# A mixture-of-experts decoder: who sends the transfers of the expert stage, and in which order

## The reference, cut to what matters

```
logits = x @ gate_w.T                       # 1024 tokens x 64 experts
topk_w, topk_idx = top_k(softmax(logits), 8)
for e in range(64):                         # w13[e]: 256 x 256, w2[e]: 256 x 128
    g = x @ w13[e][:128].T
    u = x @ w13[e][128:].T
    o = (silu(g) * u) @ w2[e].T
    out = out + combine[:, e] * o           # combine: topk_w where e was chosen
x = layernorm(x + out)
```

## Time and profile before

| | |
|---|---|
| time, median of 3 runs | 886.04 us (884.73 to 886.28) |
| profiled execution | 880.95 us, span 879.3 us |
| mean granted TensorE clock in it | 0.961 of full speed |
| PE busy | 791.1 us, 90% |
| ACT busy | 385.3 us, 44% |
| expert stage, first to last transposes of rows | 630.4 to 831.0 us |

### The profile page before, as it was taken

One profiled execution on the slowest core, in us unless ns is written; L12 is line 12 of the kernel. 1 busy time (PEld: TensorE's weight loads), 2 busy tenths in 40 slices (PEclk: granted clock), 3 DMA queues, 4 the chain that ended last, 5 costly groups with the idle time before them and its releaser, 6 DMA issues.

```text
span 879.3 us, 17480 instructions
## 1 busy us (share of the span) xinstructions
PE 791.1 (90%) x5756; PEld 663.4 (75%) x5763; DVE 547.4 (62%) x1778; ACT 385.3 (44%) x1147; POOL 322.8 (37%) x399
## 2 busy tenths in 40 slices
PE   6999998988999999999959998983399999899958
PEld 4677776766898989898936776662299999799846
DVE  2877777854666666666684688773166666555514
ACT  3445545532443434343426766651144444344434
POOL 1121112121232121212112367777366666566611
PEclk8999999999999999999987999996599999999979
DMA  9534400001121213120003244722358999955373
GB/s 257 146 115 138 132 9 13 7 1 37 43 85 42 84 44 111 43 66 25 13 10 111 72 150 139 260 81 102 116 169 287 303 297 292 323 166 167 117 308 129
DMA packets 62680, 110.16 MB, mean 125 GB/s; under 512 B 11243, under 2 KB 41433, under 8 KB 61312
## 3 DMA queue, kind: packets, MB, share of 16 engines
q1 hardware_dynamic: 40464, 73.14, 26.0%
q10 hardware_dynamic: 12960, 18.57, 6.9%
q0 software_dynamic: 9168, 17.35, 5.4%
HBM read 94.50 MB, written 35.52 MB: 148 GB/s over the span
## 4 chain that ended last, share of the span: by engine, by line
PE 79%; DVE 5%; DMA 5%; issue 4%; POOL 4%; ACT 2%; SPq 1%; DVEq 0%; POOLq 0%
PE ps L165 72%; PE ps L168 6%; DMA rows_e<-x_slots 2%; POOL x_slots L1493 2%; DMA dnb_sb<-in_dnb 1%; POOL y_slots L1854 1%; DMA rowso<-y_slots 1%; DVE topc L1382 1%; DVE pTc L1394 0%; SPq L1697 0%; DVE stats L1043 0%; DVE oT L1024 0%; ACT o_hi L961 0%; DMA x_slots<-rows_all,index_all 0%; DVE x_all L1040 0%
## 5 line engine op out<-in xcount | busy, mean ns | idle before, releaser
L1854 POOL DMA_INDIRECT y_slots<-o_e,index_e x127 | 125.0, 984 | 87.2 <-issue 58.8
L165 PE MATMUL ps<-xT_e,w_slot 128*128 128x128 f32 x760 | 100.6, 275 | 0.3 <-ACT xT_e L1793 0.2
L165 PEld LDWEIGHTS ps<-xT_e,w_slot 128*128 128x128 f32 x760 | 92.4, 192 | 1.0 <-ACT xT_e L1793 0.5
L165 PEld LDWEIGHTS ps<-diagc,softc 128*128 128x128 f32 x512 | 64.1, 204 | 33.8 <-POOL diagc L1502 24.2
L1835 DVE TENSOR_TENSOR h_e<-ps,gate_e 128x128 f32<-128x128 f32 x127 | 37.0, 291 | 81.1 <-ACT gate_e L1799 81.1
L1793 ACT COPY xT_e<-ps 128x256 f32<-128x256 f32 x127 | 47.3, 372 | 79.6 <-PE ps L168 77.7
L1340 ACT ACTIVATE softc<-ps,topc 128x256 f32<-128x256 f32 x128 | 59.0, 476 | 47.1 <-DVE topc L1382 41.5
L165 PE MATMUL ps<-diagc,softc 128*128 128x128 f32 x512 | 70.3, 294 | 8.6 <-DVE pTc L1394 4.9
L168 PE MATMUL ps<-ident,rows_e 128*128 128x128 f32 x254 | 49.7, 278 | 25.2 <-DMA rows_e<-x_slots 24.6
L1493 POOL DMA_INDIRECT x_slots<-rows_all,index_all x64 | 63.8, 997 | 18.0 <-issue 15.9
L168 PEld LDWEIGHTS ps<-ident,rows_e 128*128 128x128 f32 x254 | 35.4, 143 | 38.9 <-DMA rows_e<-x_slots 27.0
(11 more groups left out here) (271 smaller groups left out, 1869.8 us busy)
## 6 DMA issues: line engine op xcount, KB each, us to landing
w_slot<-in_we SPq DMA_DIRECT2D x71, 384.0 KB
rows_e<-x_slots SPq DMA_DIRECT2D x69, 136.0 KB
w_slot<-in_we ACTq DMA_DIRECT2D x24, 384.0 KB
x_slots<-blank SPq DMA_DIRECT2D x4, 2176.0 KB, 8.9
rowso<-y_slots SPq DMA_DIRECT2D x8, 1024.0 KB, 13.1
rows_e<-x_slots ACTq DMA_DIRECT2D x58, 136.0 KB
w_kept<-in_we SPq DMA_DIRECT2D x20, 384.0 KB, 4.3
wh<-in_wqkv SPq DMA_DIRECT2D x16, 384.0 KB, 3.6
```

The lines of the kernel that those rows point to most:

```text
L165: return self.pe.matmul(out, lhsT, rhs, start=start, stop=stop, skip_group_check=shared)
L1854: pool.indirect_dma_start(m.y_slots, bass.IndirectOffsetOnAxis(ap=T.index[:, :], axis=0), T.o[:, :], None, bounds_check=TOK * TOPK - 1, oo ...
```

## The change

All issues of the expert stage move to SP. ACT waits for no transfer of its own and sends nothing. SP's loop goes over the tiles: at j it sends the rows of tile j+5, whatever the kind, and then the weights whose buffer is freed by tile j-4 or earlier (`+ 4 <= j`), whatever the kind. The plan is waited for by the first issue that needs a register (`line_of`), and a register, once loaded, is used for both transfers of the tile.

```diff
-AHEAD = 8
...
@@ sp_experts
     for j in range(WORK):
         load_rows(t, sp, j, own_rows(m, j))
-    sp.wait_ge(*tp.lines_set(1))
-    todo = [j for j in LOADS if ORDER[j] >= NE]
-    for j in range(PLANNED - 3, TILES):
-        while todo and LOADS[LOADS.index(todo[0]) - SLOTS] + AHEAD <= j:
+
+    def line_of(j):
+
+        if j not in place:
+            if not place:
+                sp.wait_ge(*tp.lines_set(1))
+            place[j] = sp.value_load(r.extra_row[0:1, ORDER[j] - NE:ORDER[j] - NE + 1])
+        return place[j]
+
+    todo = LOADS[SLOTS:]
+    for j in range(1, TILES + 1):
+        ahead = j - 1 + WORK
+        if ahead < TILES and ORDER[ahead] < NE:
+            load_rows(t, sp, ahead, own_rows(m, ahead))
+        elif ahead < TILES:
+            at = line_of(ahead)
+            load_rows(t, sp, ahead, m.x5_slots[bass.ds(at, P), :], cond=at < NE * ROWS)
+        while todo and LOADS[LOADS.index(todo[0]) - SLOTS] + 4 <= j:
             k = todo.pop(0)
-            at = place[k] = sp.value_load(r.extra_row[0:1, ORDER[k] - NE:ORDER[k] - NE + 1])
-            load_weights(t, sp, k, a["we"][bass.ds(at // ROWS, 1), :, :].rearrange("a p n -> (a p) n"), cond=at < NE * ROWS)
-        if ORDER[j] >= NE:
-            at = place.pop(j)
-            load_rows(t, sp, j, m.x5_slots[bass.ds(at, P), :], cond=at < NE * ROWS)
+            if ORDER[k] < NE:
+                load_weights(t, sp, k, own_weights(a, k))
+            else:
+                at = line_of(k)
+                load_weights(t, sp, k, a["we"][bass.ds(at // ROWS, 1), :, :].rearrange("a p n -> (a p) n"), cond=at < NE * ROWS)
...
@@ act_experts
-def act_experts(m, a, t, tc):
-
+def act_experts(m, t):
     act = m.act
     act.preload_act_table(ACT.Silu)
-    for k in range(PARTS):
-        act.wait_ge(*tc.row_out[k](NSEQ * TOPK // PARTS))
-    todo = [j for j in LOADS[SLOTS:] if ORDER[j] < NE]
     for j in range(TILES + 1):
...
-        ahead = j - 1 + WORK
-        if WORK <= ahead < TILES and ORDER[ahead] < NE:
-            load_rows(t, act, ahead, own_rows(m, ahead))
-        while todo and LOADS[LOADS.index(todo[0]) - SLOTS] + 5 <= j:
-            k = todo.pop(0)
-            load_weights(t, act, k, own_weights(a, k))
```

More of the change, by code:

```diff
@@ L1992, in program_pe, with program_act @@
     pe_combine(m, s.to, s.te)
-def program_act(m, a, s, out):
+def program_act(m, s, out):
     act_layer0(m, s.t0, s.t1)
@@ L1999, in program_act @@
     act_cross1(m, s.tc, s.r, s.t1)
-    act_experts(m, a, s.te, s.tc)
+    act_experts(m, s.te)
     act_combine(m, s.to, s.te, s.r, out)
@@ L2060, in decoder @@
         program_pe(m, s)
-        program_act(m, a, s, out)
+        program_act(m, s, out)
         program_dve(m, s)
```

## The result

The changed kernel takes 881.61 us (median of 6 runs, 878.16 to 883.3), the one before 886.16 us on the same chips (6 runs). The ratio is 0.995, 95% interval 0.9927 to 0.9972: faster, by 2.5 to 6.5 us. The forecast was 884.5 with a range from 882.2 to 888.2: right in direction, too small in size, and outside the range. The direction was no strong claim either: "faster" had a chance of 0.41, "same" 0.42.

What follows compares the result with a forecast made beforehand. PE bounds the kernel, so transfers count only where PE stands; the expert stage loses 5.8 us. Plan's wait +1.4, dense stretch -2.1 and end -0.8 give -1.5 us: 884.5 from a median of 886.04, range 882.2 to 888.2.

Steps and rivals of the forecast that it cites:

- The plan's wait: Tile 15: its rows wait on SP behind the plan; stall 2.0 us, net +1.4 without tile 20's 0.6.
- The catch-up behind it: Tiles 16 to 20: rows regain their lead after tile 15's stall; slack grows from tile 17, tile 20 no longer waits.
- The dense stretch: Tiles 69 to 86: issues some 2.5 us earlier cut stalls of 3.4 us to 1.3, a gain of 2.1.
- the queue grows by 0.45 us each: Dense stretch: for 12 tiles transfers outlast PE's step, adding 5.4 us to a 4.3 us load, leaving a 1.5 us stall.
- The rate of 333 GB/s: Dense stretch: DMA rate at full share, giving 2.0 us for a tile's 0.66 MB against 1.55 us of PE.
- full gain: Rival, chance 0.19: dense stretch needs no wait (3.4), end gives 0.8, tile 15 stalls 1.7; -3.1 us, 882.9.
- bytes bind: Rival, chance 0.15: DMA bytes keep the dense stretch's stalls, only tile 15's shows anew; +0.6 us, 886.6.
- The end: Late in the expert stage: a long step at 815 (0.3) and a wait for ACT's copy at 824.82 (0.5) go; gain 0.8.
- The sum: Whole kernel: plan's wait +1.4, dense stretch -2.1, end -0.8, together -1.5 us.
- The rival of the clock drop: Tile 15: costlier stall or idle time lowering the clock, 1.7 us of work; full price +3.2, 889.2; chance 0.16.
- One queue or two: Dense stretch: rows on ACT's queue may overtake SP's weights, so one queue would gain less; covered by the 0 end.
- SP's time: Dense stretch: SP's issues for five tiles take some 6.6 us against PE's 7.7; fits with little idle, priced at nothing.

Runs made afterwards that it cites:

- e10: Changed kernel, SP sending no weights before j = 14, then at most one tile's a turn: stage 195.7 us, ratio to before 0.9949.
- e15: Changed kernel, but ACT sends the rows of K and L tiles: stage 195.8 us, run without a ratio.
- e5: Changed kernel again, unaltered: ratio to before 0.9965 (0.9939 to 0.9991), stage 198.7 us.
- e11: Kernel before, but SP sends the next X tile's rows ahead of weights: stage 199.0 us, ratio 0.9989 (0.996 to 1.0019).
- e14: Kernel before, but SP sends the weights of L tiles in its own loop: stage 199.2 us, run without a ratio.
- b1: Kernel before again, unaltered, run for its trace: one execution of 892.84 us, stage 202.7 us.
- e1: Changed kernel again, unaltered, while the kernel before was slow (about 915 us): ratio 1.004 (1.0003 to 1.0076), stage 227.8 us.
- e4: Kernel before, X rows sent ahead of weights by SP, in the slow condition: stage 229.6 us, ratio 1.0013.
- e6: Changed kernel, no weights before j = 14, then one tile's a turn, in the slow condition: stage 228.6 us, ratio 1.0001.
- e9: Changed kernel, K and L rows sent by ACT, in the slow condition: stage 226.0 us, ratio 0.9989.
- e12: Kernel before, L weights sent by SP, in the slow condition: stage 224.5 us, ratio 1.0046.
- e13: Changed kernel, K and L rows sent by ACT, in the slow condition: stage 226.0 us, ratio 0.9986.
- e16: Kernel of e10 with + 6 in place of + 4 (weights two steps later), in the slow condition: stage 234.2 us, ratio 0.9997.
- e17: Kernel of e10 once more, in the slow condition: stage 227.8 us, ratio 0.9969.
- e3: Kernel before, L weights sent by SP, in the slow condition: stage 225.4 us, ratio 1.0026.
- e7: Kernel before, L weights sent by SP, in the slow condition: stage 224.8 us, ratio 0.9967.

## Why the forecast fell short

*The plan's wait* was right in place, cause and size: 1.9 us for 2.0, and e10 and e15, which take the rows of 15 to 19 away from behind it in two different ways, are both rid of it. Net of the 0.6 that went at tile 20 it costs 1.3 (forecast 1.4). The catch-up behind it has less room than I gave it: in the trace after the rows of tiles 17 and 19 landed 0.5 us before their transposes, and e5 lost another 1.1 at tile 19.

*The dense stretch* is the step that failed, in size: the forecast charged 1.3 us of the 3.4 to bytes ("the queue grows by 0.45 us each", for twelve tiles), and PE lost nothing there, in four traces out of four (after, e5, e10, e15). The queue did not grow from tile to tile. Take as landing of a load the last update of its semaphore in the trace. In the trace after, the weights of tiles 74 to 77 were 3.8 to 4.5 us under way, those of 79 to 86 4.7 to 5.9 us and without a trend. These landed 1.55 us apart, as fast as PE goes, and 1.6 to 2.0 us before PE's first matmul with them. Why the time under way rose once, at tile 78 (5.5 us), and then held is not shown. But two terms of the 0.45 were off. The rate of 333 GB/s came from a stretch with late issues. In the trace after the engines moved 383 GB/s (last number) while these tiles were loaded:

```profile
757.00:770.00 13.00, 13.00 (x102) 12.10 (x102) 8.23 (x55) 5.47 (x17) 8.14 (x9) 1.00 1.03 383
```

And a tile writes less than 128 KB, since only the rows chosen for an expert are written: POOL's queue moved 17.35 MB in the whole run (packets, MB, share of the engines),

```profile
q0 software_dynamic: 9168, 17.35, 5.4%
```

of which the scatter of 8192 rows to `x5_slots` is 8.9, so a tile writes 66 KB on average; by the packets of this window it was 88 KB. By these two a tile needs 0.62 MB and 1.6 us, and hardly any queue builds up. Averaged over the 43 us of the stretch the rate at full share was still 338/0.97 = 348 GB/s: the rate has to be read where loads queue all the time. The room is thin all the same: in e5 the same loads were 6.2 to 7.1 us under way and landed 0.5 to 1.1 us before their need.

What made the stalls took both halves: rows in time alone leave PE standing for weights (e11), weights in time alone for rows (e14), both together for nothing (changed kernel past tile 19, e10, e15). In the trace of before the rows of tile 77, for which PE had been waiting 0.6 us, landed at 751.58, and the weights of tile 76, which PE wants 0.4 us later, at 751.94: had the rows been in time, PE would have waited for these. In the dense stretch the rows alone win 0.2 us of the 3.5 lost in the profile of before, the weights alone 1.2, both together all; b1 lost 5.6 there, so how the gain divides is not shown any finer. My rival "full gain" had this mechanism and was given 0.19; "bytes bind" is refuted for this stretch by the four traces without a stall.

*The end* was right by chance: the 0.8 is gone, but b1, e11 and e14 did not have it either, although ACT sends there too; it was an accident of one execution.

*The sum.* In the pair of traces: +1.3-3.4-0.8 = -2.9, which is the stage's difference. The comparison says -4.5, from -6.5 to -2.5; the second -3.1. Note that a sum with the dense stretch right, -2.9 or 883.1, still lies inside the stated range; what took the measured 881.61 below it is the 1.6 us between 2.9 and 4.5. That is not shown to be anything but scatter, with one lean: the profiled execution of before was a mild one, 880.95 us where the median was 886.04, and b1 (892.84), a bad one, lost 2.1 us more in the same stage, with a clock drop in it. The forecast took the stalls of one execution for the typical ones; what is typical these two traces do not show.

*The clock.* The rival of the clock drop did not come true: after the 1.75 us at tile 15 the clock stayed at 1.00; after the 2.1 of b1 it fell. The rival compared PE's busy time in 3 us, 1.46 before the fall in the earlier trace rows. Here it was less than that, and the clock did not fall:

```profile
657.00:660.00 3.00, 1.25 (x10) 0.85 (x9) 1.14 (x7) 0.53 (x2) 1.44 (x2) 1.00 0.89 254
```

*One queue or two.* The prediction left open whether rows on ACT's own queue overtake weights on SP's. In the trace of before they did not: the rows of tile 19, sent by ACT at 654.14, landed at 660.11, after the weights of tile 22 that SP had sent at 653.61 (landed at 657.83), and were 6.0 us under way, where SP's own rows of tile 20 took 6.4. And the changed kernel without the plan's stall has the same stage with one queue for its loads (e10) and with two (e15).

*SP's time*: in the dense stretch SP issued eight loads from 746.18 to 751.66, four tiles, in 5.5 us with waits in it. It kept up, with little idle, as reckoned: the weights of tiles 76 to 79 left 0.2 to 0.4 us after the down that frees their buffer, those of 80 to 86 0.5 to 1.2 us after it.

## What to carry to other kernels

A load's place in its issuer's list is part of its latency: put issues in the order in which the engines need the data. Where PE waits for one group of loads, look how late the next group is before repairing the first: here the rows in time alone won 0.2 us, because the weights were right behind them. If a wait for late knowledge (here a plan) enters a list, all that stands behind it inherits the wait; move it behind the loads that do not need it. Where the start of the changed stage scatters by 14 us, compare the stage, not the span, and take more than one trace of the kernel before as the base of a forecast.

## What the runs showed that was not expected

Beside e1 to e4, e6 to e9, e12 and e13, and e16 and e17, the kernel before took 912 to 921 us in place of 884 to 890. In each of the twelve traces the expert stage accounts for it: 224 to 234 us in place of 196 to 203. It is not the chip for good: e12 to e17 ran on the same one, e14 and e15 undisturbed (199.2 and 195.8), those before and after them disturbed. In such a run ACT is late in many tiles, while it waits for nothing that the profile shows: in e1 50 of the 127 copies begin 0.8 to 2.9 us after their transposes. In e1:

```profile
798.66 0.38 PE L167 MATMUL ps<-ident,rows_e 128*128 128x128 f32 x2
...
800.34 0.37 ACT L1802 COPY xT_e<-ps 128x256 f32<-128x256 f32 x1 [1.64 <-PE ps L167]
```

The transposes were over at 799.04, the copy began 1.3 us later; in the changed kernel it begins 0.04 us after them. PE then waits for it, in e1 from 650 to 860 for

```profile
PE ps L164 <- ACT xT_e L1802: 14.4, 20, 1.0
```

What holds ACT up stays open. In e1 the changed kernel came out at 1.004 of the one before (1.0003 to 1.0076), so its gain is not shown for this condition. Under it the ratios of one and the same kernel differ by more than their intervals (1.0026, 0.9967 and 1.0046 for that of e3, e7, e12), so no verdict was taken from them.
